# A gated cross-attention block with routed experts on Trainium2: weighing the zero-edged feature with spread similarity rows in place of an unfolded copy

## The reference, cut to what matters

```python
emb_l = jnp.pad(embedding[:, :, :-1], ((0, 0), (0, 0), (1, 0)))
emb_r = jnp.pad(embedding[:, :, 1:], ((0, 0), (0, 0), (0, 1)))
sim = jnp.stack([_cosine_sim(embedding, emb_l), _cosine_sim(embedding, embedding),
                 _cosine_sim(embedding, emb_r)], axis=1)
att = jnp.repeat(sim, C, axis=1)                  # (B, 384, T): row i is sim row i // 128
f_pad = jnp.pad(feature, ((0, 0), (0, 0), (1, 1)))
inp_unf = jnp.stack([f_pad[:, :, k:k + T] for k in range(K)], axis=2).reshape(B, C * K, T)
out = jnp.einsum('bit,oi->bot', inp_unf * att, w_flat)   # w_flat: (128, 384), column 3 c + k
...
x = x + tanh(g_xattn[0]) * xattn(layernorm(x), ctx_4096, weight)
h = relu(hidden @ up_w) ** 2                      # 1024 -> 2048
shared_out = h @ down_w                           # 2048 -> 1024
routed_out = ((hidden @ fc1_w) @ expert_w * sum_of_top2(hidden @ gate_w)) @ fc2_w   # 512 wide
x = x + tanh(g_ffn[0]) * layernorm(shared_out + routed_out, gamma, beta)   # hidden = layernorm(x)
```

## Time and profile before

| | |
|---|---|
| median of 3 runs | 1116.44 us (1115.82 to 1119.9) |
| the profiled execution, its own time | 1118.56 us |
| its span in the profile | 1116.7 us |
| mean granted TensorE clock | 0.956 |
| TensorE busy | 1004.0 us, 90% of the span |
| block 0's first up tile begins at | 128.86 us |
| blocks 1, 2 and 3 begin at | 413.07, 655.66 and 897.75 us |

### The profile page before, as it was taken

How to read it: one execution, slowest core, us unless ns; L and a number is a source line. 1 busy time by engine, 2 the same in 40 slices (tenths; PEclk the granted TensorE clock), 3 DMA queues, 4 the chain that set the end, 5 groups by cost and what they waited for, 6 DMA issues and landing times.

```text
span 1116.7 us, 13108 instructions
## 1 busy us (share of the span) xinstructions
PE 1004.0 (90%) x4781; PEld 466.2 (42%) x4783; DVE 550.6 (49%) x991; ACT 301.2 (27%) x413; POOL 256.2 (23%) x167
## 2 busy tenths in 40 slices
PE   5695799297979999997999999987999999999996
PEld 5342344143434444443444444443444444444442
DVE  3485876567654552674354634764454622221112
ACT  4524665644211111232011121322111112220101
POOL 5211304254642103230022222320022220000120
PEclk9897799688989999999999999998999999999998
DMA  7679597753523325546232415474233222310001
GB/s 278 199 238 363 197 364 280 286 195 98 186 76 114 113 95 184 211 164 224 111 126 97 149 62 186 178 256 171 95 133 132 94 94 95 97 35 1 19 19 39
DMA packets 54348, 169.03 MB, mean 151 GB/s; under 512 B 7114, under 2 KB 7306, under 8 KB 53258
## 3 DMA queue, kind: packets, MB, share of 16 engines
q1 hardware_dynamic: 48810, 148.76, 38.0%
q10 hardware_dynamic: 5472, 19.40, 4.6%
HBM read 123.97 MB, written 37.88 MB: 145 GB/s over the span
## 4 chain that ended last, share of the span: by engine, by line
PE 64%; issue 9%; DMA 7%; DVE 7%; SPq 4%; POOL 3%; ACT 3%; DVEq 2%; POOLq 1%; ACTq 0%
PE psS L1438 28%; PE psS L1409 12%; PE psR L1409 10%; PE psR L1449 7%; PE psP L1373 5%; SPq L383 2%; DMA pair_scratch<-hid 2%; DMA u_buf<-shift_scratch 1%; SPq L386 1%; POOL f_pair L530 1%; DMA scr<-in_ctx 1%; DMA shift_scratch<-f_pair 1%; POOL scr L513 1%; PE psR L1523 1%; DMA big<-in_L_ffn_up_w 1%
## 5 line engine op out<-in xcount | busy, mean ns | idle before, releaser
L1438 PE MATMUL psS<-big,hid 128*128 128x512 f16 x1536 | 345.8, 384 | 7.8 <-ACT y L698 7.8
L1409 PE MATMUL psS<-xT,ring 128*128 128x512 f16 x960 | 221.1, 392 | 12.5 <-DMA ring<-pair_scratch 10.9
L1438 PEld LDWEIGHTS psS<-big,hid 128*128 128x128 f16 x1536 | 151.6, 99 | 191.6 <-issue 9.3
L1409 PE MATMUL psR<-xT,ring 128*128 128x512 f16 x960 | 210.8, 379 | 3.7 <-DMA ring<-pair_scratch 3.7
L1409 PEld LDWEIGHTS psS<-xT,ring 128*128 128x128 f16 x960 | 96.4, 101 | 133.2 <-issue 15.4
L522 POOL TENSOR_TENSOR y<-y,lgb 128x1024 f32<-128x1024 f32 x15 | 35.2, 2347 | 489.3 <-ACT y L690 489.3
L1409 PEld LDWEIGHTS psR<-xT,ring 128*128 128x128 f16 x960 | 93.6, 98 | 117.9 <-issue 5.6
L645 ACT ACTIVATE sd<-sd 128x1 f32<-128x1 f32 x44 | 8.9, 202 | 375.1 <-DVE sd L917 375.1
L1449 PE MATMUL psR<-w,lgb 128*128 128x512 f16 x384 | 86.0, 379 | 0.0
L1373 PE MATMUL psP<-u_buf,wx 128*128 128x512 f16 x252 | 62.0, 393 | 12.0 <-DMA u_buf<-shift_scratch 9.3
L1126 DVE SCALAR_TENSOR_TENSOR y<-psR,rw,y 128x1024 f32<-128x1024 f32 x15 | 19.2, 1282 | 102.3 <-PE psR L1449 99.8
(11 more groups left out here) (229 smaller groups left out, 999.9 us busy)
## 6 DMA issues: line engine op xcount, KB each, us to landing
ring<-pair_scratch SPq DMA_DIRECT2D x80, 512.0 KB, 5.7
shift_scratch<-f_pair SPq DMA_DIRECT2D x36, 512.0 KB, 3.8
u_buf<-shift_scratch SPq DMA_DIRECT2D x12, 1536.0 KB
work<-in_x SPq DMA_DIRECT2D x26, 512.0 KB, 5.6
big<-in_L_ffn_up_w SPq DMA_DIRECT2D x8, 1024.0 KB, 11.8
pair_scratch<-hid ACTq DMA_DIRECT2D x16, 512.0 KB, 5.1
out_rows<-y SPq DMA_DIRECT2D x15, 512.0 KB, 3.0
sim_side<-side_scratch SPq DMA_DIRECT2D x14, 512.5 KB, 4.0
```

Of the source, the lines that this page charges most:

```text
L1409: mm = pe.matmul(up_bank[t % NR], ring[:, t % NR, a, k, :], xT[:, k, b, :], start=(k == 0 and a == 0 and b == 0), stop=(k == KB - 1 and a ...
L1438: mm = pe.matmul(psS[:, HALF * h:HALF * h + HALF], hT[:, i, a, P * j:P * j + P], dn[:, i, b, HALF * h:HALF * h + HALF], start=(i == 0 and ...
```

## The change

It does six things. (1) The host lays out inputs: x rows and the attention weight in the order ORDER (channels 0 to 41, 43 to 84, 86 to 127, then 42 and 85), the context with its columns in 128 runs of 8 and the right neighbour beside them (9 x 128 per row), the up, fc1 and expert weights by tile. (2) There is no unfolding: f stands in one buffer with a zero at either edge; three tiles S_k, one for each tap, hold for each channel the similarity row that it meets, and `weigh` on GpSimd multiplies f, shifted by k, into them in place. With ORDER, each S_k is filled by a DMA of 126 partitions from three DRAM rows, each repeated 42 times, and one of 2 partitions. The weighted tiles are split (`f_his`, `f_los`, `f_lo`), and `xattn` sums all three taps in PSUM, so that `combine` is one operation for each half. (3) The context sums are plain reductions along rows (no transposes on VectorE, no `quadrant_sums`), and the cosines are made on 128 x 4 x 9 elements. (4) In blocks 1 to 3 the turn is made by a DMA transpose from a float16 pair in SBUF (`x_hi`, `x_lo`, `turn`) rather than by TensorE. (5) In block 0, TensorE reads the split tiles where they were made (seven slots), and they go to DRAM beside it for later blocks; the latent tiles' first two batches run in the set-up (LAT_AFTER). (6) `xattn` stands ahead of the shared part for j = 1 to 3 and after five chunks for j = 0; cosines come at t = 13; and the splitting of down_w starts at t = 17 in place of t = 12.

```diff
+        SIM_T = (3, 6, 9, 12)
+        COS_T = 13
+        X_T = 6
+        XATTN_AT = (5, 0, 0, 0)
...
+            def load_sims(m, j):
+                rows = sim_dram[:, bass.ds((BB * m + j) * T, T)]
+                for k, ends in enumerate((slice(0, 2), slice(0, 3, 2), slice(1, 3))):
+                    sp.dma_start(s_of(m, j)[k][0:G * GROUP, :],
+                                 rows.rearrange("g (a t) -> g a t", a=1).broadcast_to([G, GROUP, T]))\
+                        .then_inc(s_sem(m, j), 16)
+                    sp.dma_start(s_of(m, j)[k][G * GROUP:, :], rows[ends, :]).then_inc(s_sem(m, j), 16)
+
+            def turn(m, j):
+                sp.wait_ge(xp_rdy, ahead(BB * (m - 1) + j + 1))
+                sp.sem_inc(turn_begun, 1)
+                sp.dma_start_transpose(xT[:, :, :, P * j:P * j + P].rearrange("p k s t -> p (k s) t"),
+                                       x_pair.rearrange("p k s i -> p (k s i)")).then_inc(turned, 16)
...
+                for t in range(NR, UT):
+                    sp.wait_ge(up_done, ahead(UT * n + t - NR + 1))
+                    load_tile(t)
...
+                        if t == COS_T + 3:
+                            store_sims(m)
+                            first_sims(m)
...
+            def weigh(m, j):
+                q = BB * m + j
+                pool.wait_ge(f_rdy, q + 1)
+                pool.wait_ge(s_sem(m, j), sims_loads(m, j))
+                for k in T_ORDER:
+                    rows = s_of(m, j)[k]
+                    pool.tensor_tensor(rows, f_b[b_of(m, j)][:, k:k + T], rows, ALU.mult).then_inc(t_rdy, 1)
...
             def combine(m, j):
...
+                    dve.scalar_tensor_tensor(out=xh, in0=psP[:, h, :], scalar=c_x, in1=xh, op0=ALU.mult,
+                                             op1=ALU.add).then_inc(comb, 1)
...
+                for h in range(2):
+                    for k in range(G):
+                        for n, (w, v) in enumerate(((0, 0), (0, 1), (1, 0))):
+                            mm = pe.matmul(psP[:, h, :], wx[:, k, w, :], U[b][:, k, v, HALF * h:HALF * h + HALF],
+                                           start=(k == 0 and n == 0), stop=(k == G - 1 and n == 2))
+                    mm.then_inc(p_done, 1)
...
+            def first_up_half():
+                pe.wait_ge(xt_rdy, 2 * BB)
+                for t in range(LT):
+                    tile(slot(t), t, slice(PAIR, TOK)).then_inc(up_done, 1)
+                for t in range(LT, UT):
+                    pe.wait_ge(stg_rdy, t - LT + 1)
+                    pe.wait_ge(up_evac, t - NR + 1)
+                    tile(slot(t), t, slice(0, TOK)).then_inc(up_done, 1)
+                    if t == SCALE_T:
+                        norm_over_rows(WDN, 1, 4)
+                gates(0)
```

More of the change, by code:

```diff
@@ L119, in flamingo_block @@
[L119 to L129, removed]
+        f_buf = sb("f_buf", [P, T + 2], F32)
@@ L451, in down_half @@
-                for j in range(1, BB):
-                    if phase_a:
-                        phase_a_loads(m, j)
-                    else:
+                for j in range(BB):
+                    if not phase_a:
+                        if j > 0:
+                            store_out(n, j - 1)
+                        continue
+                    q = BB * m + j
+                    if j == 0:
+                        tiles, rows = ahead(UT * m), ahead(IT * m)
+                        sp.wait_ge(up_done, tiles)
+                        sp.wait_ge(h_rdy, rows)
+                        if first:
+                            for s in range(NR):
+                                sp.wait_ge(slot_out[s], 16 * ((UT - 1 - s) // NSLOT + 1))
+                        load_x(m, 2)
+                        load_sims(m, 1)
+                    else:
+                        if j < BB - 1:
+                            sims_used(m, j)
+                            load_sims(m, j + 1)
@@ L493, in _ @@
+            for k in range(4, 6):
+                load_up(k)
+            sims_used(0, 0)
+            load_sims(0, 2)
+            sp.wait_ge(w2_done, LT)
+            for k in range(6, 8):
+                load_up(k)
+            sims_used(0, 1)
+            load_sims(0, 3)
+            first_up_half()
             down_half(0, True, first=True)
@@ L747, in up_half @@
                             dn_split_hi(c)
+                if first:
+                    for s in range(NR, NSLOT):
+                        act.wait_ge(slot_out[s], 16 * ((UT - 1 - s) // NSLOT + 1))
+                if phase_a:
+                    f_his(m, 0)
             def w2_split_hi(l):
@@ L1182, in up_half @@
                     bank = up_bank[t % NR]
-                    if first and t < NR:
-                        for it in range(NR * t, NR * t + NR):
-                            tile_lo(it)
                     if t < LT:
@@ L1268, in _ @@
             x_stats_first()
+            for j in range(1, BB):
+                sums(0, j)
+            cosines(0)
             dve.wait_ge(small_in, 32)
@@ L1303, in _ @@
             dve.drain().then_inc(scale_rdy, 1)
-            xt_los(0, BB - 1)
+            for it in range(EARLY):
+                tile_lo(it)
             dve.wait_ge(w2_sq, LT)
@@ L1395, in turn_first, with tile @@
                                       scr[j % 2][:, P * (4 * h + k):P * (4 * h + k) + P], ident[:, :])
                 mm.then_inc(tr_done, 1)
-            def up_half(n, phase_a, first=False):
-                m = n + 1
-                pe.wait_ge(xt_rdy, 2 * BB * m)
+            def tile(rows, t, cols):
+                for k in range(KB):
+                    for a, b in ((0, 0), (0, 1), (1, 0)):
+                        mm = pe.matmul(up_bank[t % NR][:, cols], rows[:, a, k, :], xT[:, k, b, cols],
+                                       start=(k == 0 and a == 0 and b == 0), stop=(k == KB - 1 and a == 1),
+                                       skip_group_check=True)
+                return mm
@@ L1412, in up_half @@
[L1412 to L1421 removed]
+                    tile(ring[:, t % NR], t, slice(0, TOK)).then_inc(up_done, 1)
@@ L1422, in up_half, with gates @@
+                gates(n)
+            def gates(n):
+                if not (isinstance(n, int) and n == 0):
+                    pe.wait_ge(rw_rdy, n)
                 for j in range(BB):
```

1197 lines of the change are left out of this document (512 added, 685 removed).

## The result

The changed kernel takes 1281.95 us (median of 4 runs, 1280.38 to 1284.56) where the kernel before took 1118.17 beside it: ratio 1.147, 95% interval 1.143 to 1.150. The forecast was 1048, its range ended at 1155. The side is that of the rival *the similarity rows move on few engines*, but the time is 139 us above the 1143 that I gave it.

What follows compares the result with a forecast made beforehand. Blocks 1 and 2 were taken as matmul-bound, with set-up and block 0 losing time to waits. Terms -20 - 10 - 27 - 14 + 2 = -69 from 1118.56 gave 1049.6, 1048 us on the runs' median; range 1030 to 1155.

Steps and rivals of the forecast that it cites:

- the similarity rows move on few engines: Rival: large similarity loads, led by 3 rows, use three engines; 19.5 us a batch, +95 together, 1143 us; chance 0.33.
- landing time of the similarity loads: Blocks 1 and 2: 1.5 MB of similarities at 423 GB/s take 3.7 us; a load's landing stays below 5 us.
- Set-up: Start to tile 4: tile 4 at 142 against 152.0, -10, the softest term; under the few-engines rival, +33.
- Blocks 1 and 2: 232.4 us each against 242.4, -20 for two, with a 5 us wait before tile 17; few-engines rival +25 each.
- The batch's chain of 35: Few-engines rival, blocks 1 and 2: a batch's loads, other transfers and GpSimd's work take 35 us against 29.8, +11.
- Cover in down_half: GpSimd's weighings of 2.2 us each stay hidden: next batch's last low half at 26.5, needed at 29.8.
- The last turn: End of a block: the DMA transpose takes 6 us, landed at 26 before the next block at 29.8, so hidden.
- the turn is late: Rival: the DMA transpose comes 12 us late at three block ends, 1084 us; chance 0.07.
- Block 0, tiles 4 to 19: No round trip through DRAM; 4 us for down_w's norm: 90 us against 117.3, -27.
- Rest of block 0: Behind block 0's tiles: 130 us against 143.8, -14, with 3, 4 and 2 us charged for waits.
- splitting bounds block 0: Rival: ScalarE and VectorE can't hold 5.18 us a tile in block 0, +25, 1073 us; chance 0.10.
- Block 3: Last block: keeps its 218.9 us, its tail not touched, 0.

Runs made afterwards that it cites:

- spread kernel: Changed kernel with each large similarity load (3 DRAM rows, 42 times each) split into three loads of one row to 42 partitions: 1108.22 us, ratio 0.991 to the kernel before.
- sums first: On the kernel with its sets behind the ring tiles, VectorE combines batch j+1 before taking batch j's column-norm maxima in the set-up: 1087.93 us (one run).
- norm later: On the kernel with its sets behind the ring tiles, TensorE's matmul for down_w's norm moved from behind tile 16 to behind tile 18: 1089.94 us (one run).
- shared chunks first: On the kernel with its sets behind the ring tiles, block 0: psS evacuated before batch 1's high halves, nine down chunks before its xattn: 1093.82 us (one run).
- f early: On the sums first kernel, block 0: batch 1's x statistics and f made amid down_w's late chunks, not behind them: 1079.54 us (one run).
- kernel with its sets behind the ring tiles: The spread kernel with similarity stores and the first batch's set issued behind ring tile 19, not before tile 17: 1091.55 us, ratio 0.977 to the kernel before.

## Why the prediction was wrong

**The step that failed** is the landing time of the similarity loads. The forecast took them as spread, 3.7 us for a set at 423 GB/s and next to the 4.0 us of the earlier trace rows; measured are 79 GB/s and 23.1 us from the first issue of a set to its first use, against 10.0 with the loads spread; "Against: the broadcasts of one row to 128 partitions land in 4.0 us" compared a load with 128 leading to one with 3. The rival had the mechanism and its signs (a share of 0.2, GpSimd waiting, TensorE idle before tile 17); I gave it 0.33 and should have put it first, since the rows against it did not have its pattern. Spreading the loads brings 174 of the 234 us between forecast and result.

**The rival's own terms** were 95 and the spans say 173, from the spread kernel to the changed one; these 78 more and the 60 of the list below make the 139 by which the time is above its 1143. Set-up +33, measured 43.9. Block 0 +12, measured 32. Blocks 1 and 2 +25 each, measured 49.2 and 47.7. In these, tile 17's wait was near (19; 21.6 and 21.0 measured). The batch's chain of 35 was right only where it has no output in it (33.9, batch 1 to 2); it is 43.9 from batch 2 to 3. I had left out that GpSimd's output and keeping (8.8 us) come between weighing and release, tied there by SyncE's order too; and that SyncE is itself held, 3.9 us for the transpose and 5.3 for a small load. Each wait also slows the matmuls behind it: TensorE is busy 235.1 us in block 1 against 227.6 with the loads spread, 7.5 us that I had not counted in the +25.

**The forecast's terms, read off the spread kernel** (1108), where its assumption holds:

- *Blocks 1 and 2*: forecast 232.4, measured 234.1 and 233.1. Right in size and in place: one wait before tile 17 of 6.2 (forecast 5), none at xattn, and it goes when the sets are issued behind the ring tiles.
- *Cover in down_half*: weighings of 2.00, 2.35 and 2.35 us for my 2.2; hidden, as argued.
- *The last turn*: a landing of 5.6 us in the changed kernel and 5.1 in the spread one (I took 6), no wait at any block's start. The rival *the turn is late* falls.
- *Set-up*: tile 4 at 142 forecast, 178.1 measured, +36. My chain said 57, then 76, then 9. Measured are xattn of batch 0 at 70.3; 88.7 from there to the last column norms' end at 159.0; and 19.1 from there to tile 4, in which two scales follow each other, 6.7 us of waiting, before the second halves of the latent tiles. The column norms in the chain are worth 3 to 7 of this: four kernels without *sums first* begin tile 4 at 177.7 to 178.9, and two with it, otherwise the same up to there, at 174.4 and 171.6. The rest was read from the timeline and not taken apart by an experiment.
- *Block 0, tiles 4 to 19*: 90 forecast, 99.3 measured. The norm's wait is 12.1, not 4: VectorE is three tiles behind TensorE there, and TensorE waits in its queue. *Rest of block 0*: 130 forecast, 143.1 measured, no better than before's 143.8: waits of 4.5 and 12.2 us with slow matmuls behind them (6.7 and 6.0 for 4.0) where I charged 9 in all. Together the two terms are 22 us over, near the +25 of the rival *splitting bounds block 0*, but not by its condition that 5.18 us a tile can't be held: with the norm's matmul two tiles later, tiles 4 to 19 take 87.2 us, at a granted clock of 1.00. The norm's wait then comes back in part behind the tiles, where the written orders of VectorE, ScalarE and GpSimd put down_w's chunks, batch 1's f and the weighing one behind the other: *norm later* won 1.6, *shared chunks first* lost 2, and only *f early*, which moves work on VectorE and ScalarE themselves, shortened that stage, by 3.
- *Block 3*: 219.0, untouched.

The sum 36 + 9 + 13 + 2 is 61 with the decimals kept; less the 2 that the forecast had charged for a slower clock, which stand inside these stages, it is the 59 us between 1049.6 and the spread kernel's profiled execution (1108.50).

## What to carry to other kernels

Before a broadcast load is costed, read the outermost count of its pattern: rows of the trace with another outermost count say nothing of it, and for the two small counts tried here, 3 and 6, the engines at work were that count. Where one queue issues everything, such a load costs more than its own time, since the issuer is held and ring loads, turns and stores stand behind it. A chain through several engines is costed by what each one's written order puts between its links, not by its links alone.

## What the runs showed of the hardware

The number of DMA engines followed the outermost count in both small counts tried: 3 gave a share of 0.19 to 0.20 and 79 GB/s, 6 gave 0.39 and 154, and with 42 leading a whole set of 1.5 MB was issued, landed and first used within 10.0 us (first issue at 508.63, first weighing at 518.65, in block 1 of the kernel with its sets behind the ring tiles; 23.1 with 3 leading, 13.1 with 6). But the spread set does not come near the 423 GB/s of the earlier trace rows, by which the forecast had it in 3.7 us. From 511 to 513 of the same kernel, with nothing but the set and its small loads under way, the share is 0.93 and the rate 223 GB/s:

```profile
511.00:513.00 2.00, 2.00 (x11) 0.89 (x10) 0.14 (x1) 0.00 (x0) 0.00 (x0) 1.00 0.93 223
```

That is an estimate of 15 GB/s for an engine at work (223 over 0.93 of 16) where 3 engines had 26 each. Whether the few DRAM rows, the smaller loads or something else sets this was not tried.

The issuing engine is held behind loads with 3 leading: the 8 KB loads at L302 took 0.4 to 1.2 us as the first two and 4.7 to 6.3 as the last of a set with 3 leading (block 1), and 0.24 with the loads spread. Full queues of the three engines would explain it; no run shows them. The transposing DMA held SyncE 2.1 to 7.0 us a time, median 3.8, for a landing of 5.6 (1.5 to 6.8, median 2.8, and 5.1 with the loads spread):

```profile
L313 SPq DMA_TRANSPOSE xT<-sides x12: 2057/3840/7042, 375.7 to 1043.7; - x12
```

VectorE's small steps are not small beside GpSimd. In block 0 of the kernel with its sets behind the ring tiles, first VectorE, then GpSimd:

```profile
282.94 2.09 DVE L1011 TENSOR_SCALAR rw<-rw,coef 128x4 f32<-128x4 f32 x1
285.10 3.06 DVE L917 TENSOR_TENSOR u_buf<-sides,u_buf 128x1024 f16<-128x1024 f32 x1
288.08 1.21 DVE L917 TENSOR_TENSOR u_buf<-y,u_buf 128x1024 f16<-128x1024 f32 x1
```

```profile
282.88 2.12 POOL L509 TENSOR_TENSOR big<-big 128x1024 f16<-128x1024 f32 x1
284.96 2.12 POOL L491 TENSOR_TENSOR u_buf<-scr,u_buf 128x1024 f16<-128x1024 f32 x1
```

The same subtraction takes 3.06 us while GpSimd's runs and 1.21 once it has ended at 287.08, and four elements a partition take 2.09 (0.23 in the shortest of the line's four executions). The Trainium skill (SBUF — State Buffer, Who interferes with whom) has the two engines share a port pair that one holds for its whole instruction; this trace agrees, as 3.06 is what was left of GpSimd's 2.12 (1.98) and 1.08 more. The forecast's chains on VectorE had no such waits. In the spread kernel's set-up, while GpSimd weighs, a step of one element a partition reads so:

```profile
81.89 2.22 DVE L859 SCALAR_TENSOR_TENSOR rs<-mv,rs 128x1 f32<-128x1 f32 x1
```

The same line takes 0.16 us in the last two batches, when GpSimd has nothing to do. Three such steps are some 6 us in the chains of batches 0 and 1; how much of that reached tile 4 was not tried.
